# A step order of one stretch and the tail of the last batch, changed together in an attention kernel on one core

## The reference

```python
xn = layernorm(x)                      # without gain and offset
h  = layernorm(xn) * ln_g + ln_b
q, k, v = h @ wq + bq, h @ wk + bk, h @ wv + bv      # 16 heads of 64
scores = q @ k.T / 8;  scores[key before query] = -inf
a  = softmax(scores) @ v
r  = a @ w0 + b0 + xn                  # attention output with its residual
x1 = x + layernorm(r)                  # "norm 2" in the kernel
u  = layernorm(x1)                     # "norm 3"
gates = softmax(top 2 of (u[:, 0, :] @ router_w.T))  # from the first token of the batch
w  = u + sum over experts of gates[e] * (u @ down[e].T) @ up[e].T
out = x1 + layernorm(w)                # "norm 4"
```

## Time and profile before

| what | value |
|---|---|
| time, median of 3 runs (lowest to highest) | 982.62 us (981.31 to 984.0) |
| the profiled execution's own time | 981.79 us |
| its span in the profile | 980.0 us |
| mean granted TensorE clock | 0.996 |
| DVE busy | 636.9 us (65%) |
| ACT busy | 538.3 us (55%) |

### The profile page before, as it was taken

One profiled execution on the slowest core, in us unless ns is written; L12 is line 12 of the kernel. 1 busy time (PEld: TensorE's weight loads), 2 busy tenths in 40 slices (PEclk: granted clock), 3 DMA queues, 4 the chain that ended last, 5 costly groups with the idle time before them and its releaser, 6 DMA issues.

```text
span 980.0 us, 20358 instructions
## 1 busy us (share of the span) xinstructions
PE 946.4 (97%) x7646; PEld 596.7 (61%) x7650; DVE 636.9 (65%) x1867; ACT 538.3 (55%) x731; POOL 702.4 (72%) x517
## 2 busy tenths in 40 slices
PE   8899999999999999999999999999999999999895
PEld 4565666666666566666666656666656665665563
DVE  6676566565666857566857667666666576766367
ACT  5355656454545665664555565665546456465443
POOL 7278777666778877777777778886578777776762
PEclk9999999999999999999999999999999999999999
DMA  4000101121001111101002100011100211011110
GB/s 116 23 1 3 23 23 25 23 45 23 3 23 45 23 24 24 24 9 38 23 24 67 23 14 13 24 24 44 24 23 3 66 23 24 23 24 24 24 44 22
DMA packets 61813, 26.94 MB, mean 27 GB/s; under 512 B 39060, under 2 KB 53780, under 8 KB 61716
## 3 DMA queue, kind: packets, MB, share of 16 engines
q1 hardware_dynamic: 61696, 25.64, 11.4%
q10 hardware_dynamic: 20, 0.00, 0.0%
HBM read 22.76 MB, written 2.35 MB: 26 GB/s over the span
## 4 chain that ended last, share of the span: by engine, by line
PE 87%; DVE 5%; issue 3%; POOL 3%; ACT 2%; DMA 0%; POOLq 0%; ACTq 0%; DVEq 0%
PE po L788 24%; PE st L773 21%; PE sc L736 10%; PE st L698 9%; PE st L768 7%; PE st L854 6%; PE sc L798 3%; PE st L713 2%; PE st L714 2%; PE st L715 2%; DVE stats L1234 1%; DVE sc L1263 1%; DVE k_low L1320 1%; PE st L862 1%; ACT ring L1062 0%
## 5 line engine op out<-in xcount | busy, mean ns | idle before, releaser
L536 POOL TENSOR_TENSOR total<-total,ring 128x1024 f32<-128x1024 f32 (+1 forms) x313 | 538.9, 1722 | 238.0 <-PE po L788 198.1
L1263 DVE CUSTOM_DVE_ANT_0 sc<-sc,key_mask 128x512 f32<-128x512 f32 (+1 forms) x496 | 230.4, 522 | 107.5 <-PE sc L736 103.6
L1062 ACT ACTIVATE ring<-st 128x1024 f32<-128x1024 f32 (+1 forms) x256 | 228.5, 918 | 125.6 <-PE st L773 107.0
L1266 DVE TENSOR_REDUCE least<-sc 128x1 f32<-128x512 f32 x268 | 168.3, 671 | 70.2 <-PE sc L736 68.8
L788 PE MATMUL po<-ring,v_sb 128*64 128x512 f32 (+3 forms) x1280 | 210.7, 467 | 0.0
L773 PE MATMUL st<-q_high,k_low 64*128 64x512 f32 (+3 forms) x768 | 176.8, 447 | 0.0
L788 PEld LDWEIGHTS po<-ring,v_sb 128*64 128x64 f32 x1280 | 86.8, 137 | 129.0 <-issue 123.9
L736 PE MATMUL sc<-k_high,q_high 64*128 64x512 f32 (+3 forms) x768 | 134.4, 380 | 9.1 <-DVE least L1263 3.4
L773 PE MATMUL st<-q_low,k_high 64*128 64x512 f32 (+3 forms) x768 | 136.3, 342 | 0.0
L773 PE MATMUL st<-q_high,k_high 64*128 64x512 f32 (+3 forms) x768 | 136.2, 342 | 0.0
L736 PEld LDWEIGHTS sc<-k_high,q_high 64*128 64x128 f32 x768 | 68.5, 185 | 79.3 <-issue 61.6
(11 more groups left out here) (184 smaller groups left out, 1257.1 us busy)
## 6 DMA issues: line engine op xcount, KB each, us to landing
inv_row<-sums_dram SPq DMA_DIRECT2D x62, 256.0 KB, 4.0
x_a<-x SPq DMA_DIRECT2D x4, 512.0 KB, 5.2
sums<-sums_row SPq DMA_DIRECT2D x124, 2.0 KB, 2.1
x_b<-x SPq DMA_DIRECT2D x3, 512.0 KB, 6.0
out<-res_b SPq DMA_DIRECT2D x3, 512.0 KB, 4.9
total<-w_pairs SPq DMA_DIRECT2D x1, 1152.0 KB, 6.7
shift_row<-shift_t SPq DMA_DIRECT2D x62, 4.0 KB
x_a<-x SPq DMA_DIRECT2D x2, 256.0 KB, 3.4
```

What stands on the lines that cost most here:

```text
L536: nc.gpsimd.tensor_tensor(so_far, so_far, tile_of(n, s)[:, :, col:col + w], ALU.add).then_inc(s_add, 1)
L1062: nc.scalar.activation(tile_of(n, s)[:, :, 0:w], st[s % 2][:, :, 0:w], ACT.Exp, scale=SCALE).then_inc(s_exp, 1)
L1263: last = nc.vector.tensor_tensor_reduce(bank[:, col:col + w], bank[:, col:col + w], key_mask[:, 0:w], -1.0, 3e38, ALU.add, ALU.min, least[ ...
L1266: last = nc.vector.tensor_reduce(least[:, h, a:a + 1], bank[:, col:col + w], AX.X, ALU.max, negate=True)
```

## The change

It has two parts.

The first is one string. In stretch 0 of the slots 1 to 31 the order STSTTS becomes STTSTS. T1 goes ahead of S4. The last slot has no first scores to make, so its sequence does not change.

The second is in the tail of the last batch:

- PE projects both halves of the pair before (`out_before`) right after the first half of the last pair, and no longer the second half later on.
- ACT multiplies the first head of the second half by its reciprocals into `scaled`, a part of `inv_row`. DVE adds this tile in one instruction in place of four.
- `add_before(1)` and the reciprocals of the second half (`invert(1)`) move ahead of `residual(0)` on DVE.
- Norm 2 is no longer applied to `y_a`. `residual(a)` adds `acc` times the root to `x_a` in four instructions on DVE. The part that is missing, the moved mean, drops out of norm 3, and POOL adds it to a copy of `x_a` in `x_b` (128x512, once for each half) for the final sum.
- PE adds the identity to the product of the gated matrices by one more product into the same bank, so `project_up` gives the sum with `u`. DVE takes the statistics of norm 4 and both engines apply it straight from PE's banks; the addition of `y_a` (L1533) goes.
- The first token's tile is normed and transposed ahead of the other three of the first half. The numbers of unread products become smaller.

```diff
-    ORDER = ["STSTTS", "STTSTTS", "STSTTS"]
+    ORDER = ["STTSTS", "STTSTTS", "STSTTS"]
...
+        last_ups = [[st[0][:, 0, :], st[0][:, 1, :]], [sc[:, 1, :], st[1][:, 1, :]]]
...
+        scaled = inv_row[:, 0:HALF].rearrange("p (j e) -> p j e", e=E)
...
+            def last_first_roots(a, part):
...
+                nc.gpsimd.tensor_tensor(root, variance, minus_half[:, part, 0], ALU.pow).then_inc(s_root, 1)
+                pool.wait_ge(s_root, count)
+                pool_link(nc.gpsimd.tensor_tensor(moved, mean, root, ALU.mult))
...
+                if norm == 3:
+
+                    nc.gpsimd.tensor_tensor(x_b[:, part, :], x_a[:, part, :], moments[2][:, part, 3:4].to_broadcast([P, 4, E]),
+                                            ALU.add).then_inc(s_last_x, 1)
...
                 if a == 1:
-                    out_before(a)
...
                 if a == 0:
-                    out_before(a)
+                    for half in range(2):
+                        out_before(half)
...
-            unread(26)
-            need(s_last_n3, 1)
-            turn_four(y_a, 0, sc[:, 1, :]).then_inc(s_last_turn, 1)
+            unread(18)
+            need(s_last_token, 1)
+            nc.tensor.transpose(sc[:, 1, 0:P], y_a[:, 0, :], ident[:]).then_inc(s_last_turn, 1)
...
-            nc.tensor.matmul(st[1][:, 0, 0:E], down_sb[:], up_gated[:], start=True, stop=True).then_inc(s_last_down, 1)
+            nc.tensor.matmul(st[1][:, 0, 0:E], down_sb[:], up_gated[:], start=True, stop=False)
+            nc.tensor.matmul(st[1][:, 0, 0:E], ident[:], ident[:], start=False, stop=True).then_inc(s_last_down, 1)
...
-            apply_last(2, 0, acc[b % 2], 2, s_last_r)
-            apply_last(3, 0, x_a, 4, s_last_n3)
+            for j in range(4):
+                last = nc.scalar.activation(scaled[:, j, :], by_head[1][0][:, j * P:(j + 1) * P], ACT.Copy,
+                                            scale=inv_sums[:].rearrange("p g i -> p (g i)")[:, 8 + 2 * j:9 + 2 * j])
+            last.then_inc(s_last_scaled, 1)
...
             def residual(a):
-                if a == 0:
-                    link(apply_last(2, a, acc[b % 2]))
-                dve.wait_ge(s_last_r, a + 1)
-                link(nc.vector.tensor_tensor(rows_of(x_a, a), rows_of(x_a, a), rows_of(y_a, a), ALU.add))
+
+                dve.wait_ge(s_root, last_root(2, a))
+                for t in (low, high)[a]:
+                    last = nc.vector.scalar_tensor_tensor(out=x_a[:, t, :], in0=acc[b % 2][:, t, :], scalar=moments[2][:, t, 2:3],
+                                                          in1=x_a[:, t, :], op0=ALU.mult, op1=ALU.add)
+                link(last)
                 norm_stats(3, x_a, (low, high)[a]).then_inc(s_var, 1)
 
+            def up_stats(a):
+                dve.wait_ge(s_last_up, a + 1)
+                norm_stats(4, {4 * a + j: last_ups[a][j // 2][:, j % 2 * P:(j % 2 + 1) * P] for j in range(4)},
+                           (low, high)[a]).then_inc(s_var, 1)
+
+            wait_taken(dve, "out", N - 3, 0)
+            invert(0)
             take_out(0)
             dve.wait_ge(s_xa, 16 * B)
+            link(add_before(1))
+            invert(1)
             residual(0)
             take_out(1)
...
             residual(1)
-            apply_last(3, 1, x_a).then_inc(s_last_u, 1)
+            up_stats(0)
...
+            up_stats(1)
```

More of the change, by code:

```diff
@@ L644, in _ @@
                         normalise(t - 1)
+            def last_first_roots(a, part):
+                count = last_root(2, a)
+                mean, variance, root, moved = (moments[2][:, part, k:k + 1].rearrange("p t o -> p (t o)") for k in range(4))
+                pool.wait_ge(s_var, count - 1)
+                nc.gpsimd.tensor_tensor(root, variance, minus_half[:, part, 0], ALU.pow).then_inc(s_root, 1)
+                pool.wait_ge(s_root, count)
+                pool_link(nc.gpsimd.tensor_tensor(moved, mean, root, ALU.mult))
             for norm, a in ((2, 0), (3, 0), (2, 1), (3, 1), (4, 0), (4, 1)):
@@ L904, in fill @@
                     for a in range(2):
-                        last = project_up(a, dst[:, a * HALF:(a + 1) * HALF])
+                        last = project_up(a, [dst[:, a * HALF:(a + 1) * HALF]])
                 last.then_inc(s_fill[bank], 1)
@@ L1214, in _ @@
             nc.scalar.copy(both_ways[:], st[1][:, 0, 0:E]).then_inc(s_dg, 1)
-            apply_last(3, 1, x_a, 2, s_last_n3)
+            act.wait_ge(s_root, last_root(3, 1))
+            norm_apply(3, y_a, x_a, range(4, 6)).then_inc(s_last_n3, 1)
             take_turned(1)
             for a in range(2):
-                apply_last(4, a, y_a, 2, s_last_f)
+                act.wait_ge(s_root, last_root(4, a))
+                for j in range(2):
+                    t = 4 * a + j
+                    root, moved = root_and_moved(4, t)
+                    last = nc.scalar.activation(y_a[:, t, :], last_ups[a][0][:, j * P:(j + 1) * P], ACT.Identity, bias=moved,
+                                                scale=root)
+                last.then_inc(s_last_f, 1)
         @block.vector
@@ L1233, in norm_stats @@
                 for t in tiles:
-                    last = nc.vector.bn_stats(stats[norm][:, t, :], src[:, t, :])
+                    tile = src[t] if isinstance(src, dict) else src[:, t, :]
+                    last = nc.vector.bn_stats(stats[norm][:, t, :], tile)
                 link(last)
@@ L1493, in take_out @@
                 rows = rows_of(acc[b % 2], a)
-                for h in range(2):
+                for h in range(a, 2):
                     for j in range(4):
@@ L1528, in _ @@
             residual(1)
-            apply_last(3, 1, x_a).then_inc(s_last_u, 1)
-            for a in range(2):
-                dve.wait_ge(s_last_up, a + 1)
-                rows = rows_of(y_a, a)
-                link(nc.vector.tensor_tensor(rows, st[0][:, a, :].rearrange("p (j e) -> p j e", e=E), rows, ALU.add))
-                norm_stats(4, y_a, (low, high)[a]).then_inc(s_var, 1)
-            for a in range(2):
-                link(apply_last(4, a, y_a))
-                dve.wait_ge(s_last_f, a + 1)
-                rows = rows_of(y_a, a)
-                nc.vector.tensor_tensor(rows, rows, rows_of(x_a, a), ALU.add).then_inc(s_last, 1)
+            up_stats(0)
+            dve.wait_ge(s_root, last_root(3, 1))
+            for t in high[2:]:
+                root, moved = root_and_moved(3, t)
+                last = nc.vector.tensor_scalar(y_a[:, t, :], x_a[:, t, :], root, moved, ALU.mult, ALU.add)
+            last.then_inc(s_last_u, 1)
+            up_stats(1)
+            for a in range(2):
+                dve.wait_ge(s_root, last_root(4, a))
+                for j in range(2):
+                    t = 4 * a + 2 + j
+                    root, moved = root_and_moved(4, t)
+                    last = nc.vector.tensor_scalar(y_a[:, t, :], last_ups[a][1][:, j * P:(j + 1) * P], root, moved, ALU.mult,
+                                                   ALU.add)
+                link(last)
+                dve.wait_ge(s_last_f, a + 1)
+                dve.wait_ge(s_last_x, a + 1)
+                rows = rows_of(y_a, a)
+                nc.vector.tensor_tensor(rows, rows, rows_of(x_b, a), ALU.add).then_inc(s_last, 1)
 def kernel(**inputs):
```

69 lines of the change are left out of this document (42 added, 27 removed).

## The result

| what | before | changed |
|---|---|---|
| median of 6 runs each, one chip | 982.6 us | 975.71 us |
| lowest to highest | 981.31 to 985.45 | 973.68 to 976.56 |
| the profiled execution: time, span | 981.79, 980.0 us | 975.81, 974.1 us |
| its mean granted TensorE clock | 0.996 | 0.991 |

A forecast was written before the change was run, and what follows sets the result against it. PE, busy 97% of the span, was taken as the bound, with no engine bounding the tail. Slots 9.15 us plus tail 0.2 us gave 9.35 us, from 982.62 to 973.3 us; range 968 to 978.

The forecast's parts named there:

- The mechanism of the slots: Stretch 0: T1 ahead of S4 removes S4's wait for S3's maxima; 0.25 us in each of 27 slots, 6.75 us.
- The rival in which the wait only changes its place: Stretch 0: the 0.29 us wait stays with S4 behind T1; time within 1 us of 982; chance 0.03.
- the one in which S5 waits: Stretch 0: S5 waits for S4's first maxima instead of S4; slower, up to 990 us; chance 0.05.
- The rival in which the gain is lost behind the slots: Later steps take the slots' gain back; 978 us with half lost, 982.4 less the tail with all; chance 0.12.
- S5 to the projection: Last step of stretch 0: the projection of q follows S5 after 0.35 us, 0.37 before.
- The three slots behind a new projection input: Slots 6, 14 and 22, where DVE reaches S3's maxima late: 0.8 us gained each, 2.4 us.
- The tail: From 943 us on, a chain of DVE, POOL, ACT and PE: 0.2 us gained when held, 1.4 when not.
- DVE held: Middle of the tail: POOL's addition into `x_b` holds DVE's small operations until 968.8 us; chance 0.55.
- First half: Tail, to the first residual addition: the second half's reciprocals wait for PE's second sums; 0.2 us lost.
- Second half: Tail, to the second residual addition: four products with reciprocals leave DVE, 1.15 us; gain so far 0.9 us.
- The middle: Tail, to norm 3's last tile: between 0.5 us lost and 0.7 gained, taken as held, tile at 969.5 us.
- The end: Tail's last part: the addition ahead of the second statistics of norm 4 goes, 0.69 us gained.

The follow-up runs named there:

- e7: Changed kernel with the exponential of T0 made over half its columns in the slots from 1 on; 974.14 us, ratio 0.9917.
- e8: Changed kernel with POOL's last normalisation waiting, late second-half reciprocals, late second-half addition into `x_b` and 6 and 2 unread products; 972.87 us, ratio 0.9912.
- e9: The changed kernel again, letter for letter, on another occasion and chip; 976.74 us, ratio 0.9923.
- e4: Changed kernel with POOL's last normalisation waiting until DVE's last additions of the first half are done; 974.89 us, ratio 0.9906.
- e5: e4 with POOL's second-half addition into `x_b` moved behind the root of the first half of norm 4; 973.07 us, ratio 0.9911.
- e6: e4 with more unread products, 9 for 4 before the second transposition and 2 before the second up projection; 973.38 us, ratio 0.9917.
- e11: e8 with the first half's addition into `x_b` also moved behind the root of the first half of norm 4; 972.72 us, ratio 0.9883.
- e10: The kernel before with only the new order string of stretch 0, run again beside e9; 976.29 us, ratio 0.9917.
- e1: The kernel before with only the order string of stretch 0 changed, nothing of the tail; 977.57 us, ratio 0.9937.

## Why the prediction was right, and where its sum was off

**The mechanism of the slots** was right. S4 no longer waits for S3's maxima. It stands at T0 + 1.85 (forecast 1.86), T2 at T0 + 2.22 (2.23) behind ACT's exponential, S5 0.94 behind it (0.93). The rival in which the wait only changes its place falls with this, and so does the one in which S5 waits. But S5 had 0.04 us to spare by e7, and not the 0.1 that I had worked out. The rival in which the gain is lost behind the slots falls too: the stretch from T7 of one slot to T0 of the next is the same within 0.02 us.

**The step in it that was mis-sized** is the last one, S5 to the projection. I took 0.35, and it is 0.39, as in the earlier trace rows and not better. So a slot gains 0.21 and not 0.25. The three slots behind a new projection input gained 0.71, 0.69 and 0.70, not 0.8: S5 waits there for S4's maxima, 0.14 to 0.18 us and not 0.1. The sum is 7.7 us in the first trace, and 6.9 to 7.1 in eight of the nine other traces with the new order and a whole exponential (7.65 in e8), against a forecast of 9.15. This difference, 1.5 to 2.2 us, is most of what the forecast had too much. The gap between 7.7 and 6.9 is there with identical code (changed kernel and e9), in steps of 0.05 to 0.07 us in single slots. Its cause is open.

**The tail** was forecast at 0.2 us gained, DVE held. The table counts from T7 of slot 31 and gives the gain against the kernel before at four points, summed up from the start. e4 is the fair comparison: no collision, and TensorE at the lower level for about 3 us, as before.

| ends at | before | forecast | e4 | e9 | first trace |
|---|---|---|---|---|---|
| residual addition, first half | +13.89 | -0.2 | +0.09 | +0.78 | -2.49 |
| residual addition, second half | +24.02 | +0.9 | +1.22 | +1.91 | -1.35 |
| last tile of norm 3 on DVE | +27.63 | -0.5 | +0.19 | +0.89 | -2.37 |
| last addition | +35.94 | +0.2 | +0.38 | +0.90 | -2.19 |

- First half: in e4 the reciprocals wait 1.07 us for the second sums, as forecast, and these end at +12.49 where I had +12.69. The 0.2 lost become nothing. In e9 the sums end at +10.91 and nothing waits for them, with PE at the full level all the while. In the first trace they end at +15.06 and the wait is 2.40 us.
- Second half: between the first two rows the forecast has 1.1 and the traces 1.13 to 1.14. This term is right.
- The middle: forecast 1.4 lost when held, measured 1.02 to 1.03. The held case is the one that came, with 0.95 us for a small operation beside POOL's addition. That addition took 1.05 and not the 1.28 of the earlier trace rows, which is most of the difference.
- The end: forecast 0.7 gained for the addition that goes, measured 0.01 to 0.19. This step failed. The addition is gone, but PE stands idle 2.10 us before the second half is turned, and its up projection runs at the lower level. In the first trace it takes 2.08 us from 964.62 on, where it took 1.16. I had looked at DVE's row alone here. Where this projection ran at the full level (e5, e6, e8, e11), the stretch from the last tile of norm 3 to the last addition is 7.20 to 7.37 us against 8.31 before, so the gain is there once the clock is.

That e4 comes out at 0.38 us where the sum says 0.2 is luck: its terms were off by +0.3, 0, +0.4 and -0.5 us and cancel.

**What I had not seen at all** is the collision between POOL's normalisation and DVE's additions at the start of the tail, which costs 1.0 us by itself (e7 against e4), and 2.45 to 3.1 us with what the clock did in those executions (e10 against e1, the first trace against e9). It was in the program before, too. In the first trace the tail took back over a quarter of the slots' gain. Together: 7.70 - 2.19 = 5.51 of the two distances, with 0.44 that came ahead of slot 1, is the 5.9 us between the two spans. The medians are 6.9 us apart. The changed kernel came out 2.4 us above the single number and inside the range. Of this, 1.5 to 2.2 us are the slots, and the rest is within what the collision and the clock do to single executions.

## What to carry to other kernels

When a step's order in a pipelined loop is changed, work out who releases each of the moved steps in the new place, and by how much the next limit is behind: here half an exponential less left T0 to the projection at 3.55 us, since DVE's maxima let S5 come only 0.04 us earlier. In a tail that no engine bounds, read the clock of the matrix engine and the neighbours of every two-input instruction on DVE before an edit is priced, and look at a second execution of the same code before a loss in one trace is put down to the edit. An instruction given to an idle POOL is not free: put it where DVE waits for PE, as in e11.

## What the hardware showed that I had not expected

**The clock of the tail.** Windows of 2 us in the kernel before, where PE's row shows no idle time (columns as above, PEclk behind POOL's):

```profile
943.00:945.00 2.00, 2.00 (x20) 1.94 (x16) 1.53 (x2) 0.93 (x2) 2.00 (x2) 0.95 0.00 0
945.00:947.00 2.00, 2.00 (x17) 1.81 (x17) 1.34 (x4) 0.61 (x2) 1.28 (x2) 0.50 0.00 0
947.00:949.00 2.00, 2.00 (x12) 1.70 (x12) 1.73 (x7) 2.00 (x6) 0.00 (x0) 0.70 0.00 0
```

TensorE fell to the 1.2 GHz level at about 944.8 us, at the end of 16 products with one column each (943.07 to 945.11), without having been idle. In the changed kernel's first trace, with 0.94 us idle ahead of these products, it was at that level from about 937 to 944 us, in e10 from 939 to 946, in e4 without any idle time from 940 to 943, and in the first 12 us of the tail of e9, e6 and e11 not at all. The first sums took 1.95 us at the full level and up to 2.72 below it. The same code (e9 and the first trace) can thus get either. Why is open.

**The scatter of the runs follows the granted clock.** The kernel before took 981.17 to 981.62 us in the eight runs of the three occasions with a mean clock of 0.998, and 984.65 to 985.34 in the nine with 0.993. Compared at 0.993 the order alone gives 7.0 us (977.74 to 978.17 in its five runs), as much as its slots. How far the collision makes this scatter is not settled. e4, in which it can't occur, still scatters from 972.98 to 975.45.
